# One weight pair loaded later, and parts of a row addition spread over VectorE's and GpSimd's programs in a spiking feed-forward kernel

## What is computed

```python
def _L0_cond_ref(inputs, initial_state):          # inputs = x (2, 2048, 512), initial_state (2, 512)
    rates = jax.nn.relu(inputs) * DT              # DT = 0.001
    c = initial_state[:, None, :] + jnp.cumsum(rates, axis=1)
    fl = jnp.floor(c)
    prev = jnp.concatenate([jnp.floor(initial_state)[:, None, :], fl[:, :-1, :]], axis=1)
    return (fl - prev) / DT

def _L0_ffn_ref(x, w1, b1, w2, b2):               # w1 (512, 2048), w2 (2048, 512)
    h = jax.nn.relu(jnp.einsum('bsd,dw->bsw', x, w1) + b1)
    return jnp.einsum('bsw,wd->bsd', h, w2) + b2

x = x + _L0_ffn_ref(_L0_cond_ref(x, cond_1024), w1, b1, w2, b2)
```

## Time and profile before

| | |
|---|---|
| median of 3 runs | 105.36 us (105.01 to 106.45) |
| profiled execution | 105.21 us, of which the trace's span is 103.5 us |
| TensorE busy | 88.1 us |
| VectorE busy | 67.2 us |
| GpSimd busy | 46.6 us |
| ScalarE busy | 35.4 us |
| DMA, mean over the span | 288 GB/s |

### The profile page before, as it was taken

How to read it: one execution, slowest core, us unless ns; L and a number is a source line. 1 busy time by engine, 2 the same in 40 slices (tenths; PEclk the granted TensorE clock), 3 DMA queues, 4 the chain that set the end, 5 groups by cost and what they waited for, 6 DMA issues and landing times.

```text
span 103.5 us, 1028 instructions
## 1 busy us (share of the span) xinstructions
PE 88.1 (85%) x299; PEld 44.0 (43%) x299; DVE 67.2 (65%) x161; ACT 35.4 (34%) x64; POOL 46.6 (45%) x47
## 2 busy tenths in 40 slices
PE   5999999999999999999999979998999999800000
PEld 5934444444644424551544344437964454200000
DVE  2529899999498968899898967699993030003100
ACT  2867525325075550579550000068950000000000
POOL 6598000000047600027452812599940578568850
PEclk9999999999999999999999999999999999995555
DMA  2999999999999999951019997457999999999781
GB/s 74 250 367 410 426 412 412 410 410 405 410 409 410 401 389 391 407 218 10 6 21 187 182 326 314 124 155 304 418 424 412 405 421 372 208 210 142 88 132 35
DMA packets 9019, 29.77 MB, mean 288 GB/s; under 512 B 2040, under 2 KB 2168, under 8 KB 7831
## 3 DMA queue, kind: packets, MB, share of 16 engines
q1 hardware_dynamic: 6192, 25.43, 63.0%
q0 software_dynamic: 2672, 4.22, 21.9%
q10 hardware_dynamic: 146, 0.01, 0.1%
HBM read 21.58 MB, written 10.75 MB: 312 GB/s over the span
## 4 chain that ended last, share of the span: by engine, by line
PE 59%; POOL 17%; issue 10%; DVE 7%; POOLq 3%; DVEq 0%
PE ps_table L877 48%; POOL out L373 9%; POOL x_sb L380 6%; PE ps_small L988 4%; DVE same L657 3%; PE ps_idle L893 3%; DVE x_sb L749 2%; POOLq L61 2%; PE ps_turn L914 2%; POOLq L280 1%; POOL out L426 1%; POOL general_x L415 1%; DVE is_first L664 1%; PE ps_idle L903 1%; PE ps_turn L926 1%
## 5 line engine op out<-in xcount | busy, mean ns | idle before, releaser
L877 PE MATMUL ps_table<-w_sb 128*128 128x512 f32 x128 | 58.7, 607 | 0.0
L877 PEld LDWEIGHTS ps_table<-w_sb 128*128 128x128 f32 x128 | 23.9, 195 | 27.7 <-issue 26.4
L368 POOL DMA_INDIRECT rates<-in_x_turned,sixteen_at x8 | 8.7, 1089 | 32.0 <-DVE sixteen_at L618 30.2
L604 DVE SCALAR_TENSOR_TENSOR total_two<-x_sb,total_two 128x1024 f32<-128x1024 f32 x14 | 17.1, 1224 | 1.8 <-DMA x_sb<-in_x 1.5
L469 ACT ACTIVATE w_sb<-w_sb,b_col 128x512 f32<-128x512 f32 (+2 forms) x19 | 12.2, 643 | 16.3 <-DMA w_sb<-in_w_pairs 16.2
L373 POOL DMA_INDIRECT out<-w_sb,to_single x8 | 12.7, 1582 | 8.6 <-issue 7.0
L983 PE MATMUL ps_met<-w_sb 128*128 128x512 f32 x32 | 14.2, 596 | 0.0
L470 ACT ACTIVATE w_sb<-w_sb,minus_relu_b 128x512 f32<-128x512 f32 (+2 forms) x19 | 12.3, 649 | 0.6
L749 DVE TENSOR_TENSOR x_sb<-x_sb,ps_idle 128x2048 f32<-128x2048 f32 x5 | 11.1, 2281 | 0.2 <-DVE others_turn L712 0.2
L380 POOL TENSOR_TENSOR x_sb<-x_sb,idle_row 128x512 f32<-128x512 f32 x8 | 10.0, 1276 | 1.0 <-DVEq L788 1.0
L983 PEld LDWEIGHTS ps_met<-w_sb 128*128 128x128 f32 x32 | 5.9, 190 | 6.7 <-issue 6.5
(11 more groups left out here) (143 smaller groups left out, 82.1 us busy)
## 6 DMA issues: line engine op xcount, KB each, us to landing
x_sb<-in_x SPq DMA_DIRECT2D x16, 512.0 KB, 14.7
out<-x_sb SPq DMA_DIRECT2D x8, 1024.0 KB, 6.5
w_sb<-in_w_pairs SPq DMA_DIRECT2D x15, 512.0 KB, 16.1
x_sb<-idle_row POOLq DMA_DIRECT2D x1, 1024.0 KB, 8.6
w_sb<-in_w_pairs SPq DMA_DIRECT2D x2, 256.0 KB, 2.8
b_row<-in_b SPq DMA_DIRECT2D x1, 256.0 KB, 14.7
rates<-in_x_turned,sixteen_at POOLq DMA_INDIRECT x8, 4.3
out<-w_sb,to_single POOLq DMA_INDIRECT x8, 5.9
```

The source lines that it names most:

```text
L368: pool.indirect_dma_start(out=rates[:, col, :], out_offset=None, in_=x_sixteen, in_offset=bass.IndirectOffsetOnAxis(ap=sixteen_at[:, col:c ...
L604: chain(dve.scalar_tensor_tensor(out=total_two[b][:, :, :], in0=tokens, scalar=0.0, in1=total_two[b][:, :, :], op0=ALU.max, op1=ALU.add))
L877: last = pe.matmul(ps_table[c][:, :], table_hidden[:, m, c * P:(c + 1) * P], w2_sb[:, m, :], start=(m == 0), stop=(m == FC - 1))
```

## The change

- SyncE loads pair 10 behind x's last two pieces, as the first of the pairs that follow them, where it stood ahead of them.
- GpSimd adds tokens (1,12,14), two where it was one, and does it ahead of `get_rows(0)`, so that this `get_rows(0)` now also stands behind the wait for `reading_psum` at 1. Its later part has six tokens where it had seven.
- VectorE adds quarter (0,4,8) behind `find_tokens(1)`, ahead of `list_rows(0)` and `count_met(1)`; quarter (0,8,12) between `find_leads(1)` and `find_slots(1)`; quarter (0,12,16) behind `find_row_tokens`. Behind `turn_others` it has two quarters left, where it had five.
- TensorE's parts of table chunks 12 to 15 are laid otherwise around the small steps. No matmul is added or taken away.

```diff
             load_pair(9)
             load_x(13)
-            load_pair(10)
             load_x(14)
             load_x(15)
-            for m in range(11, FC):
+            for m in range(10, FC):
                 load_pair(m)
...
             for q in range(JOINED):
                 join_idle(q)
+            pool.wait_ge(reading_psum, 1)
+            add_idle(1, 12, 14)
             get_rows(0)
-            pool.wait_ge(reading_psum, 1)
-            add_idle(1, 12, 13)
             get_rows(1)
             pool.wait_ge(reading_psum, 2)
-            add_idle(1, 13, 16)
+            add_idle(1, 14, 16)
             add_idle(1, 8, 12)
...
             find_tokens(1)
+            add_idle(0, 4, 8)
             list_rows(0)
             count_met(1)
             find_leads(1)
+            add_idle(0, 8, 12)
             find_slots(1)
             list_rows(1)
             find_row_tokens()
+            add_idle(0, 12, 16)
             find_odd()
...
             turn_others()
             dve.sem_inc(reading_psum, 1)
-            add_idle(0, 4, 8)
-            add_idle(0, 8, 12)
-            add_idle(0, 12, 16)
             add_idle(1, 0, 4)
             add_idle(1, 4, 8)
...
             list_rows(0)
-            table_part(12, 0, 1)
             spread_tokens(1)
-            table_part(12, 1, DC)
-            table_part(13, 0, 2)
+            table_chunk(12)
+            table_part(13, 0, 3)
             count_leads(1)
-            table_part(13, 2, DC)
+            table_part(13, 3, DC)
+            table_part(14, 0, 3)
             list_rows(1)
-            table_part(14, 0, DC)
+            table_part(14, 3, DC)
+            table_part(15, 0, 1)
             spread_row_tokens()
-            table_chunk(15)
+            table_part(15, 1, DC)
             first_layer()
```

## The result

The changed kernel took 108.1 us in the median (107.15 to 109.12, 4 runs) against 105.19 (104.87 to 106.45): a ratio of 1.019, with a 95% interval of 1.014 to 1.024. The ratio compares undisturbed runs alone, two of the four of the changed kernel, so it is smaller than the quotient of the medians. The profiled execution took 107.15 us with a span of 105.3. The forecast was 103.0 with a range from 102.2 to 105.4.

A forecast was written before the change was run, and what follows sets the result against it. DMA stores, then GpSimd's scatters, were taken to bound the tail. The general scatter at 96.7 in place of 98.95, 2.25 earlier, took the profiled 105.21 to 102.96, forecast 103.0 us, range 102.2 to 105.4.

The forecast's parts named there:

- What bounds the kernel: Tail: paced by DMA first, with 7 stores of 8 packed behind 69.7, then by GpSimd's scatters; TensorE has room.
- VectorE's quarters: VectorE: three quarters move earlier, no work saved; is_first 0.7 us less, slots 2.9 later, last two quarters 72.35 to 76.8.
- Pair 10 at no price: Loads: pair 10 comes 2.6 us later, at 40.1, and the delay is hidden.
- its cover: TensorE: pair 10 is turned by 41.6 and taken at 43.33, a cover of 1.7 us.
- The gathers: GpSimd's gathers meet stores (0,0) and (0,1): second of b = 0 lands at 69.5, first layer starts at 74.6.
- The bound that I had taken from the gathers of rates: Gathers: beside a filled queue 4.0 us more, so the second of b = 0 lands at 70.8 at latest.
- GpSimd's tokens: GpSimd: six tokens run from 72.35 to 79.85, first scatter at about 79.9 and not 81.31, a gain of 1.4.
- The clock: TensorE: a 4 us gap probably lowers the clock; price between nothing and 3.9 us, taken as 1.6.
- the first of the signs: TensorE ahead of the first layer: a gap much beyond 4 us would show the forecast wrong.
- The sum: End: row_ready at 96.7 against GpSimd at 96.3; general scatter at 96.7 in place of 98.95, 103.0 us.
- rival (3): Gathers and clock at full price: first layer at 79.9, 3.9 of clock, time 110.6, or 106.8 halfway; chance 0.10.

The follow-up runs named there:

- one_quarter: Kernel before with VectorE's (0,4,8) moved behind list_rows(0) and GpSimd's two tokens put in count_met(1), gathers' order untouched: 104.05 us, 0.984.
- pair_alone: Kernel before with pair 10's load moved behind x's last pieces and nothing else: 106.33 us, 1.0097.
- Runs 2: Changed kernel with the second store, (0,1), held until both gathers of b = 0 have landed: 109.65 us, 1.033.
- 3: Changed kernel with VectorE's list_rows(0) ahead of its first quarter and GpSimd's get_rows(0) ahead of the wait for reading_psum: 106.03 us, no interval.
- pool_alone: Kernel before with GpSimd's edits only, two tokens and the wait for reading_psum ahead of get_rows(0): 105.55 us, 0.997.
- kept_warm: Changed kernel with 60 extra matmul calls on TensorE ahead of the first layer: 111.39 us, 1.059.
- warm_30: Changed kernel with 30 extra matmul calls on TensorE ahead of the first layer: 106.35 us, 1.004.
- second_held: Changed kernel with list_rows(0) and get_rows(0) first, pair 10 early, and store (0,2) held until the last gather landed: 107.54 us, 1.018.
- two_matched: Changed kernel with list_rows(0) and get_rows(0) first, pair 10 early, and (0,12,16) behind turn_others again: 104.03 us, 0.976.
- two_quarters: one_quarter with (0,8,12) moved too, between find_leads(1) and find_slots(1), TensorE's parts as before the change: 104.65 us, 0.979.
- copy_later: pair_alone with ScalarE's copy of the idle base and idle row behind its last table chunk: 106.14 us, 1.003.

## Why the prediction was wrong, point by point

**What bounds the kernel.** Right. Stores sent earlier do bring the end forward: one_quarter gains 1.6% by one of them.

**VectorE's quarters.** Right in length (2.29 each), and is_first at 0.16. All of it stands 0.6 to 1.0 us later than forecast: the first quarter at 55.98 for 55.0, `count_met(1)` at 58.78 for 57.9, the slots at 64.95 for 64.1, the last two quarters from 72.91 for 72.35. Behind this is the late idle sum of the next point: TensorE's count for b = 0 stands behind it, VectorE waited 2.10 us for that, and the table ended at 71.55 for 70.6.

**Pair 10 at no price.** Wrong. I named its cover, which held (it was turned from 40.19, forecast 40.1), and missed that something else goes with the load order: TensorE's signal for the idle sum, which brought the idle row 1.4 us later in pair_alone's profile (0.3 to 1% of the time in the two kernels that had the late pair and nothing else of the change) and 1.3 us in the changed kernel's. There it is the likely reason why the gathers of b = 0 go at 61.44 and 62.83 and not at 60.5 and 61.8.

**The gathers: the step that failed.** I named the collision, but took 69.5 for the second gather of b = 0, 7.7 us behind its issue at 61.8, and let the last gather go in the same moment. It went at 72.81, 3.3 us later. The gather was issued 1.0 later, at 62.83; it landed after 9.2 us and not 7.7 (1.5); and from the landing to GpSimd's next issue 0.8 us pass, which I had put at nothing. Then the last gather took 5.8 and not 5.0 (0.8), and the first layer started at 78.70 and not at 74.6, 4.1 in all. The bound that I had taken from the gathers of rates, 4.0 us lost, was nearly right: it lost 4.2. My working inside it, two stores and then 2.6 us for the gathers' own bytes, was too short. Runs 2, 3 and pool_alone show the cause from three sides: with the second store held the same gather lands after 5.0 us; issued ahead of the stores, the rows are no longer waited for; with the same order but one store it lands after 6.6. The wait for these rows accounts for 3.4 us of the 8.2 by which the first layer is late against the kernel before; 4.0 are the late row numbers, of which I had forecast 2.8, and 0.8 the last gather's.

The Trainium skill's rule that I cited, DMA: Bandwidth & Descriptors (Queues, rings and completion order), gave an estimate of 2.6 to 4.9 us for one turn of waiting (it takes a packet of the profile for a descriptor, which no run shows). q0 had no packet from 61.5 to 67, until 5.6 us behind the issue of the first gather and 4.2 behind that of the second, near the estimate, and 78.70 lies within the 73.3 to 80.8 that I gave by that rule (4.9 us lost in both waves would make its upper end 81.7; 80.8 is a slip of mine). Behind the turn both queues moved at once, 40.1% for q0 and 55.6% for q1 from 67 to 70.6.

**GpSimd's tokens.** I let six tokens start with `reading_psum` at 72.35 and forgot what stands ahead of them: `get_rows(1)`, which ended at 73.80. They started 1.5 us later than forecast, 0.6 of it by VectorE and 0.9 by the gather, and the first scatter went at 81.37, where it had been before; the forecast gain of 1.4 was gone. Only the gone wait ahead of the fifth scatter, issued at 90.14 for 91.32, was left.

**The clock.** Right in kind: 2.0 us, shown by kept_warm. That my 1.6 lies near it is luck in part, a choice between nothing and 3.9 that no row had narrowed; what sets it is that the clock stays at 1.2 GHz for 4.2 us of the layers' work. The gap was 7.15 us and not 4, the first of the signs that I had named for being wrong.

**The sum.** `row_ready` let the last scatter go at 101.35, forecast 96.7: 4.1 us from the first layer, 0.4 from the clock, 0.2 behind it. The tail behind it was 3.95 us for 4.5, which leaves 107.15 for 103.0. That is rival (3), *slower*, in its place and past its point (`row_ready` behind 98.95, first layer behind 76.9), to which I gave a tenth. It was likelier than I put it, because the two waves are coupled: the first wave's delay is the second wave's issue time.

## What to carry to other kernels

A transfer that becomes ready earlier is not free: list what else is in the DMA queues in the stretch it moves into, above all small gathers that an engine waits for, and send those first. When a producer works on its own schedule, price an added wait by everything in its program behind it, gathers and the next waits on them included. And where an edit opens a gap on TensorE, count the lower clock behind it. Filling the gap with idle matmuls made the layers 1.6 to 2.5 us shorter here; in the time of the whole only warm_30 against the changed kernel shows it, 1.5%.

## What the runs showed of the hardware

- The last gather of w1 rows lands 4.3 to 5.1 us behind its issue in the six kernels with no store under way then, after 5.6 to 7.0 in ten of the eleven kernels in which one store or two were moving beside it (8.0 in warm_30's slowest execution), and after 11.9 with two stores just ahead of it and a third close behind. The second gather of b = 0 took 9.2 to 10.1 in the four kernels with two stores issued just ahead of it.
- GpSimd's next gather starts 0.7 to 0.8 us behind the landing that it waits for.
- A VectorE instruction on two SBUF inputs stands for as long as GpSimd's additions run, also through two of them back to back: 0.16 us alone, 0.88 beside one and 2.30 beside two. With an input from PSUM: 0.75 in either case.
- TensorE's clock fell to 1.2 GHz during an idle gap of 7.15 us, and the layers behind it took 2.0 us longer. Behind gaps of 2.9 us (second_held, warm_30) and 3.6 (two_matched) it was still at 2.4 GHz when work resumed and fell within that work; the layers took 1.6 us longer. In two_quarters it fell after waits of 1.55, 0.43 and 0.34 us within 5 us.
- TensorE's signal behind a matmul can come 2 us after the matmul's modelled end: in all eight kernels with pair 10 loaded late and in one of ten with it early. copy_later shows that it is the signal and not ScalarE. Its cause is open.
